# Selective scan: three of sixteen products with C on GpSimd, step sizes summed by TensorE, B's rows spread by DMA, eight states in the ring

## The chip, the cores and the metric

The kernel runs on one core of one Trainium2 chip. The metric is the device time of the whole program in microseconds (us); before the change the median of three runs is 4557.76 us (4557.75 to 4559.65). Engines are named as the profile names them: PE is TensorE, PEld its weight load, DVE is VectorE, ACT is ScalarE, POOL is GpSimd, SP is SyncE, which issues the transfers.

## The reference, cut to what matters

The program is a chain of eleven phases (three attentions, two mixtures of experts, two recurrent networks, norms, and one selective scan). Only the scan is touched. Its arithmetic, with 16 batch elements of 512 tokens, 256 inner channels and 16 states per channel:

```python
xz = jnp.einsum('btd,ed->bte', x, in_proj_w)
xi, z = jnp.split(xz, 2, axis=-1)
xc = _silu(causal_depthwise_conv(xi) + conv_b)
x_dbl = jnp.einsum('bti,ei->bte', xc, x_proj_w)
dt_lo, Bp, Cp = jnp.split(x_dbl, [DT_RANK, DT_RANK + D_STATE], axis=-1)
dt = jax.nn.softplus(jnp.einsum('btr,ir->bti', dt_lo, dt_proj_w) + dt_proj_b)
A = -jnp.exp(A_log)
def step(h, inp):
    dt_t, B_t, C_t, x_t = inp
    dA = jnp.exp(dt_t[..., None] * A[None])
    dBx = dt_t[..., None] * B_t[:, None, :] * x_t[..., None]
    h = dA * h + dBx
    y_t = jnp.sum(h * C_t[:, None, :], axis=-1)
    return (h, y_t)
y = scan(step) + Dp * xc
y = y * _silu(z)
return jnp.einsum('bti,di->btd', y, out_proj_w)
```

## The kernel before, in words

Two functions make the selective scan. `mamba_in` goes over the 16 batch elements, makes xc, silu(z), the raw step size and the 32 rows of B and C, and stores them to DRAM; B and C are stored as three bf16 parts whose sum is the f32 row (`high`, `middle`, `low`). `mamba_scan` then loads one batch element after another and runs 16 states n = 0 to 15 for each. Channels are the partitions, in two halves of 128 that lie side by side in a tile of 1024 columns (2 halves of 512 tokens). For state n of batch element b:

- PE spreads row n of B over 128 partitions (`broadcast_b`, L2247, into the PSUM tile `b_ps`), ACT copies it to SBUF (`copy_b`, L2323, `b_sb`).
- POOL multiplies it with dt*x, one instruction per half (L2449, `dbx`, ring of R = 4).
- ACT makes exp(dt*A) for both halves (L2363, `da`, ring of 2 in PSUM).
- DVE runs the recurrence with one scan instruction (L2498, `state`, ring of RS = 4).
- PE spreads row n of C (`broadcast_c`, L2253, one PSUM tile `c_ps`); it may do so once DVE has read the row before.
- DVE multiplies state and C (`times_c`, L2506, `prod`, ring of 2), one state behind the scan.
- PE adds the product to `y_ps` with a product with the identity matrix (`sums`, L2271).

Beside these, once per batch element: ACT and POOL make the next element's step size (six ACT instructions per half, L2330 to L2354, then `lose`, `mend`, `step_size` on POOL, L2422 to L2432) and POOL scales x by it (L2439); PE adds D*x to y at n = 9 and 11 (L2295); DVE gates y (L2515); PE multiplies by the output weights and adds the residual (`outward`, L2262 and L2263, at n = 4, into the same PSUM tile as B's rows); ACT copies the result (`take_sum`, L2350).

Each engine runs its own list in the order in which it is written in `sequence`; semaphores order the engines among each other. The order around the change is set by the constants at the head of `mamba_scan` and by the `if n == ...` lines in each `sequence`. Transfers are issued by SP in the order of `load`.

Of the kernel before, what the change touches and what calls it, by code (L numbers as in the profile page):

```python
# [1967 lines left out]
def mamba_in(core, xn, mamba_dram, bc_dram, w):  # L1968
# [7 lines left out]
    with core.phase() as ph:  # L1976
# [16 lines left out]
        STORES = 4  # L1993
# [7 lines left out]
        def _(pe):  # L2001
# [40 lines left out]
        def _(act):  # L2042
# [47 lines left out]
        def _(dve):  # L2090
# [11 lines left out]
            def copy_dbl(n):  # L2102
                dve.wait_ge(dbl_mm, n + 1)
                if n >= 1:
                    dve.wait_ge(dt_mm, 2 * n)
                dve.tensor_copy(dbl[:, :], dbl_ps[0:BC + RANK, :]).then_inc(dbl_copied, 1)

            def rest_of(n):
# [3 lines left out]
                dve.tensor_tensor(rest[:, :], dbl_ps[0:BC, :], high[:, n % OB], ALU.subtract).then_inc(rest_ready, 1)  # L2112
# [25 lines left out]
        def _(sp):  # L2138
            def store(n, u):
                sp.dma_start(mamba_dram[n].rearrange("k p t -> p k t"), out[:, u]).then_inc(stored[u], 16)  # L2140
                for r, part in enumerate((high, middle, low)):
                    sp.dma_start(bc_dram[n, r], part[:, u]).then_inc(stored[u], 16)
# [9 lines left out]
def mamba_scan(core, x, mamba_dram, bc_dram, w):  # L2152
# [5 lines left out]
    RS = 4  # L2158
    RP = 2
    RA = 2  # L2160
    RB = 8
    AHEAD = 6
    COPIED = 4
    AT = 4
    SKIP_AT = (9, 11)
    OUT_AT = 4
    with core.phase() as ph:
        inp = ph.sb("inp", [P, 2, KINDS, T])
        bc = ph.sb("bc", [3 * BC, 2, T], BF16)
# [6 lines left out]
        b_sb = ph.sb("b_sb", [P, RB, T])  # L2176
        skip_w = ph.sb("skip_w", [P, 2, P])
        dbx = ph.sb("dbx", [P, R, 2 * T])
        state, prod = ph.sb("state", [P, RS, 2 * T]), ph.sb("prod", [P, RP, 2 * T])
        gated = ph.sb("gated", [P, 2, T])  # L2180
        da = ph.ps("da", [P, RA, 2 * T])
        b_ps, c_ps = ph.ps("b_ps", [P, T]), ph.ps("c_ps", [P, T])
        y_ps = ph.ps("y_ps", [P, 2, T])
        out_ps = b_ps
        loaded = [ph.sem(f"loaded{u}") for u in range(2)]
        step_loaded = [ph.sem(f"step_loaded{u}") for u in range(2)]
        select_loaded = ph.sem("select_loaded")
# [14 lines left out]
        acc_mm = ph.sem("acc_mm")  # L2202
# [8 lines left out]

        @block.sync
        def _(sp):
            def load(b, u):
                sp.dma_start(inp[:, u, 4:6], mamba_dram[ds(b, 1), 4:6].rearrange("a k p t -> (a p) k t")
                             ).then_inc(step_loaded[u], 16)
                sp.dma_start(bc[:, u], bc_dram[ds(b, 1)].rearrange("a r c t -> (a r c) t")).then_inc(loaded[u], 16)
                sp.dma_start(inp[:, u, 0:4], mamba_dram[ds(b, 1), 0:4].rearrange("a k p t -> (a p) k t")
                             ).then_inc(loaded[u], 16)

            load(0, 0)
            sp.dma_start(w["select"], w["select_dram"]).then_inc(select_loaded, 16)
# [12 lines left out]
        def _(pe):
            pe.sem_inc(acc_mm, 2 * RP)
            pe.sem_inc(out_mm, 1)

            def inputs_loaded(b, u):
                pe.wait_ge(loaded[u], 32 * (b // 2) + 32 if isinstance(b, int) else 16 * (b - u) + 32)  # L2240

            def broadcast_b(b, u, n):

                if n == 0:
                    inputs_loaded(b, u)
                pe.wait_ge(b_ready, STATE * b + n + 1)
                pe.matmul(b_ps[:, :], w["select"][:, n], bc[:, u], start=True, stop=True).then_inc(b_mm, 1)  # L2247

            def broadcast_c(b, u, n):
                if n == 0:  # L2250
                    inputs_loaded(b, u)
                pe.wait_ge(prod_ready, RS + STATE * b + n)
                pe.matmul(c_ps[:, :], w["select"][:, STATE + n], bc[:, u], start=True, stop=True  # L2253
                          ).then_inc(c_mm, 1)

            def outward(b, follows=True):

                pe.wait_ge(gated_ready, 2 + 2 * b + 2)
                pe.wait_ge(added, b + 1)
                pe.wait_ge(b_ready, 1 + (STATE * (b + 1) + OUT_AT + AHEAD + 1 if follows else STATE * (b + 1)))  # L2260
                for h in range(2):
                    pe.matmul(out_ps[:, :], w["out_w"][:, h], gated[:, h], start=(h == 0), stop=False)  # L2262
                pe.matmul(out_ps[:, :], w["ident"], tok(x, b), start=False, stop=True).then_inc(out_mm, 1)  # L2263

            def sums(b, n, first):
                m = STATE * b + n
# [492 lines left out]
```

## Time and profile before

| | |
|---|---|
| median of 3 runs | 4557.76 us |
| the profiled execution, its own time | 4557.68 us |
| its span, first to last instruction | 4555.9 us |
| busy in the span: PE, DVE, ACT, POOL | 86%, 71%, 65%, 52% |
| `mamba_in` | up to 1172 us |
| `mamba_scan`: first scan, last scan | 1192.81 us, 2059.69 us |

Busy shares are means over eleven phases with different limits, so the stage of the change is read by itself: the busy times of the engines from 1193 to 2066 us, then the groups of instructions in it, then the instructions in order of time. A duration is that of one instruction alone; where instructions of one engine follow each other without a gap, the distance from start to start is what one costs, and it is somewhat shorter than its duration.

### The profile page before, as it was taken

What the parts mean: (1) busy time and instruction counts of PE and PEld (TensorE: products, weight loads), DVE (VectorE), ACT (ScalarE), POOL (GpSimd) and SP (SyncE); (2) the same over time, 40 slices, a digit from 0 to 9 for tenths busy, and PEclk for the clock granted to TensorE, in tenths of its full rate; (3) what the DMA queues carried; (4) which work ended last, traced back from release to release, by engine and by line L of the source; (5) the groups of instructions that cost most, each with busy time, mean ns of one, the idle gap of its engine ahead of it and who ended that gap; (6) DMA issues with size and microseconds to landing.
All of it is one profiled execution on the core that took longest, in us unless ns stands there. A gap on an engine that the chain in (4) does not pass through costs nothing. (4 is left out here: it accounts for less than half of the span.)

```text
span 4555.9 us, 92840 instructions
## 1 busy us (share of the span) xinstructions
PE 3902.2 (86%) x30083; PEld 1984.7 (44%) x30084; DVE 3239.7 (71%) x7596; ACT 2951.3 (65%) x5997; POOL 2373.4 (52%) x2953
## 2 busy tenths in 40 slices
PE   7599999899677777779879999996988699997897
PEld 4244444463222222226423333335984244443896
DVE  3588888448799999994459999982116688887013
ACT  7488888767666666666758888883334477775332
POOL 3266666211688899980321545454544336665452
PEclk9799999999899999999979999998998799998997
DMA  9533333004310000000263333334655534442666
GB/s 279 166 90 86 86 87 88 23 0 162 110 40 34 29 29 29 29 15 0 103 200 88 91 88 90 89 83 138 211 191 194 173 107 118 115 113 81 198 215 197
DMA packets 500325, 486.05 MB, mean 107 GB/s; under 512 B 160194, under 2 KB 434755, under 8 KB 499808
## 3 DMA queue, kind: packets, MB, share of 16 engines
q1 hardware_dynamic: 481744, 443.29, 32.4%
q0 software_dynamic: 18160, 37.42, 2.3%
q8 instruction: 230, 3.77, 0.4%
q14 instruction: 191, 1.56, 0.1%
HBM read 321.07 MB, written 159.42 MB: 105 GB/s over the span
## 5 line engine op out<-in xcount | busy, mean ns | idle before, releaser
L1668 ACT ACTIVATE p_probs<-p_t_ps 128x512 f32<-128x512 f32 (+1 forms) x2048 | 1028.9, 557 | 345.8 <-PE p_t_ps L1427 149.4
L1448 PE MATMUL p_o_ps<-p_probs,p_v_st 128*32 128x256 f32 (+3 forms) x9728 | 749.8, 381 | 10.8 <-ACT p_o_sb L1630 10.1
L1761 DVE TENSOR_REDUCE p_row_max<-p_s_ps 128x1 f32<-128x512 f32 x1024 | 632.8, 678 | 56.2 <-PE p_s_ps L1376 56.1
L2449 POOL TENSOR_TENSOR p_dbx<-p_dtx,p_b_sb 128x512 f32<-128x512 f32 x512 | 635.7, 1274 | 42.8 <-DVE p_state L2498 40.0
L1376 PE MATMUL p_s_ps<-p_s_k,p_s_q 48*128 48x512 bf16 (+3 forms) x3072 | 607.0, 335 | 49.0 <-DVE p_row_max L1758 35.1
L2498 DVE TENSOR_TENSOR_SCAN p_state<-p_da,p_dbx 128x1024 f32<-128x1024 f32 x256 | 584.7, 2284 | 21.0 <-issue 18.1
L1409 PE MATMUL p_t_ps<-p_t_q,p_t_k 50*128 50x512 bf16 (+3 forms) x3072 | 545.2, 333 | 50.1 <-DMA p_t_q<-shifts 20.0
L1758 DVE CUSTOM_DVE_ANT_0 p_tried<-p_s_ps,c_mask_row 128x512 bf16<-128x512 f32 (+3 forms) x1024 | 441.2, 485 | 85.4 <-PE p_s_ps L1376 78.0
L1758 DVE CUSTOM_DVE_ANT_0 p_tried<-p_s_ps,p_s_bias 128x512 bf16<-128x512 f32 (+3 forms) x1024 | 441.6, 481 | 82.1 <-PE p_s_ps L1376 80.4
L1312 POOL TENSOR_TENSOR p_probs<-p_probs,xn 128x384 f32<-128x384 f32 (+1 forms) x384 | 408.8, 1092 | 153.9 <-ACT p_probs L1666 153.6
L2271 PE MATMUL p_y_ps<-p_prod,c_ident 128*128 128x512 f32 x1024 | 484.4, 595 | 3.4 <-DVE p_gated L2515 3.4
L802 POOL DMA_INDIRECT weighed_rows<-p_y,p_raw x284 | 271.8, 957 | 291.4 <-DVE p_y L790 246.9
L790 DVE TENSOR_TENSOR p_y<-p_out_ps,p_raw 128x256 f32<-128x256 f32 x142 | 60.3, 425 | 503.4 <-PE p_out_ps L741 503.4
L772 ACT ACTIVATE p_hidden<-p_hid_ps 128x512 f32<-128x512 f32 x284 | 169.6, 597 | 316.3 <-PE p_hid_ps L730 316.3
L1409 PEld LDWEIGHTS p_t_ps<-p_t_q,p_t_k 50*128 50x128 bf16 x3072 | 166.8, 93 | 462.5 <-ACT p_probs L1668 229.9
L2363 ACT ACTIVATE p_da<-p_dt,p_rate 128x512 f32<-128x512 f32 (+1 forms) x512 | 330.6, 680 | 10.4 <-DVE p_state L2498 10.4
L2323 ACT ACTIVATE p_b_sb<-p_b_ps 128x512 f32<-128x512 f32 x256 | 152.2, 594 | 283.9 <-PE p_b_ps L2247 245.4
L1448 PEld LDWEIGHTS p_o_ps<-p_probs,p_v_st 128*32 128x32 f32 x9728 | 194.1, 108 | 309.6 <-issue 256.1
L1376 PEld LDWEIGHTS p_s_ps<-p_s_k,p_s_q 48*128 48x128 bf16 x3072 | 213.6, 95 | 221.4 <-DVE p_row_max L1761 123.4
L2506 DVE TENSOR_TENSOR p_prod<-p_state,p_c_ps 128x1024 f32<-128x1024 f32 x256 | 306.3, 1196 | 0.5 <-PE p_c_ps L2253 0.5
L593 POOL DMA_INDIRECT routed_rows<-p_rows,p_index x256 | 251.8, 984 | 100.2 <-issue 72.9
L1303 POOL COPY p_v_st<-p_v_raw 128x128 f32<-128x128 f32 x192 | 55.7, 290 | 434.5 <-PE p_o_ps L1448 258.1
(308 smaller groups left out, 7205.3 us busy)
## 6 DMA issues: line engine op xcount, KB each, us to landing
p_wb<-in_w SPq DMA_DIRECT2D x142, 512.0 KB, 3.6
p_s_q<-stack_q SPq DMA_DIRECT2D x384, 96.0 KB, 2.3
p_s_k<-stack_k SPq DMA_DIRECT2D x384, 96.0 KB, 2.4
p_t_q<-stack_q SPq DMA_DIRECT2D x384, 96.0 KB
p_t_k<-stack_k SPq DMA_DIRECT2D x384, 96.0 KB
mamba_inputs<-p_out SPq DMA_DIRECT2D x16, 1536.0 KB, 5.6
p_raw<-routed_rows SPq DMA_DIRECT2D x142, 130.0 KB, 3.1
stack_q<-p_parts SPq DMA_DIRECT2D x48, 384.0 KB, 2.8
```

The lines of the kernel that those rows point to most:

```text
L1312: pool.tensor_tensor(tile, tile, bias["t_whole"][:, 4 * g + j, first - c * P:first - c * P + width], ALU.add).then_inc(t_biased, 1)
L1376: mm = pe.matmul(s_ps[:, slot, at:at + width], s_q[rows, g % 2, pair, c * P:(c + 1) * P], s_k[rows, g % 2, pair, 0:width], start=True, sto ...
L1409: mm = pe.matmul(out[r], t_k[rows, g % 2, pair, c * P:(c + 1) * P], t_q[rows, g % 2, pair, first:first + width], start=True, stop=not mask ...
L1448: mm = pe.matmul(o_ps[32 * j:32 * j + 32, at:to], v_st[:, g % 2, c, j, :], probs[:, g % 2, j, place[c] + at - first:place[c] + to - first] ...
L1668: act.activation(exps, tile, ACT.Exp, scale=scale).then_inc(expd, 1)
L1758: read = dve.tensor_tensor_reduce(tried[:, slot, at:at + width], scores, over, 1.0, LOWEST, ALU.add, ALU.max, found)
L1761: read = dve.tensor_reduce(found, scores, X, ALU.max)
L2271: pe.matmul(y_ps[:, h], w["ident"], prod[:, n % RP, half(h)], start=(n == 0), stop=(n == STATE - 1)).then_inc(acc_mm, 1)
L2363: act.activation(da[:, n % RA, h * T + h:h * T + T], dt[:, u, h, h:T], ACT.Exp, scale=rate[:, h, n:n + 1]).then_inc(da_ready, 1)
L2449: pool.tensor_tensor(dbx[:, n % R, half(h)], dtx[:, u, h], b_sb[:, n % RB], ALU.mult).then_inc(dbx_ready, 1)
L2498: dve.tensor_tensor_scan(out=state[:, n % RS], data0=da[:, n % RA], data1=dbx[:, n % R], initial=0.0, op0=ALU.mult, op1=ALU.add).then_inc( ...
L2506: dve.tensor_tensor(prod[:, n % RP].rearrange("p (h t) -> p h t", h=2), state[:, n % RS].rearrange("p (h t) -> p h t", h=2), c_ps[:, :].un ...
```

## The change

In `mamba_in` the rows of C alone are split into three bf16 parts; B and C are stored as f32 rows too (one more store, of `dbl`, which becomes a ring). In `mamba_scan`:

- B's rows come by transfers that read four rows of DRAM and write them to all 128 partitions (`load_b`, 1 MB each, four per batch element); `broadcast_b` and `copy_b` are gone.
- The products with C of the states 1, 6 and 11 (`BY_POOL`) are done by POOL, four states behind its own multiplication with B (`times_c` in its list), with rows of C that a transfer spreads (`load_c`, three of 256 KB). PE adds them three states later (`pool_sums`). DVE and `broadcast_c` leave these states out.
- The ring of states has eight places instead of four.
- The step size is a sum of four terms made by PE with the identity matrix (`step_sum`, four products per half at n = 5 and n = 7, into one PSUM tile that `outward` uses too); ACT copies it (`take_step`, at n = 9 and 11). `lose`, `mend` and `step_size` are gone from POOL. ACT's six instructions per half move from n = 4 to 11 to n = 0 to 6; `outward` moves from n = 4 to n = 3.
- SP's list is written out over the 16 batch elements, with a wait ahead of most transfers.

```diff
-    RS = 4
+    RS = 8
     RP = 2
     RA = 2
+    QUAD = 4
+    RB = 2 * QUAD
     SKIP_AT = (9, 11)
-    OUT_AT = 4
+    OUT_AT, TAKEN_AT = 3, 7
+    DT_AT, DT_COPIED_AT = (5, 7), (9, 11)
+    SCALED_AT = (13, 15)
+    BY_POOL = (1, 6, 11)
+    POOL_BEHIND, POOL_SUM_BEHIND = 4, 3
...
+            def load_steps(b):
+                if b >= 2:
+                    sp.wait_ge(above_ready, 2 * (b - 1))
+                sp.dma_start(inp[:, b % 2, 4:6], mamba_dram[b, 4:6].rearrange("k p t -> p k t")
+                             ).then_inc(step_loaded[b % 2], 16)
...
+            def load_c(b):
+                if b >= 1:
+                    sp.wait_ge(pool_prod_ready, K * b)
+                for j, n in enumerate(BY_POOL):
+                    sp.dma_start(c_sb[:, j], rows_dram[b, n:n + 1].to_broadcast([P, T])).then_inc(c_loaded, 16)
+            def load_b(b, q):
+                no = STATE // QUAD * b + q
+                if no >= 2:
+                    sp.wait_ge(dbx_ready, 2 * QUAD * (no - 1))
+                at = STATE + QUAD * q
+                sp.dma_start(b_sb[:, QUAD * (q % 2):QUAD * (q % 2) + QUAD].rearrange("p n t -> p (n t)"),
+                             rows_dram[b, at:at + QUAD].rearrange("n t -> (n t)").unsqueeze(0).to_broadcast([P, QUAD * T])
+                             ).then_inc(b_loaded[q % 2], 16)
+            load_steps(0)
+            load_steps(1)
+            load_inputs(0)
+            load_b(0, 0)
+            load_b(0, 1)
             sp.dma_start(w["select"], w["select_dram"]).then_inc(select_loaded, 16)
+            load_c(0)
+            load_inputs(1)
+            for b in range(NB):
+                if 1 <= b and b + 1 < NB:
+                    load_steps(b + 1)
+                load_b(b, 2)
+                if 1 <= b and b + 1 < NB:
+                    load_inputs(b + 1)
+                load_b(b, 3)
+                if b + 1 < NB:
+                    load_b(b + 1, 0)
+                    load_b(b + 1, 1)
+                    load_c(b + 1)
...
+            def step_sum(b, h):
+                pe.wait_ge(back, 4 * b + 2 * h + 2)
+                pe.wait_ge(soft, 1 + 6 * b + 3 * h + 3)
+                pe.wait_ge(above_ready, 2 * b + h + 1)
+                terms = (lost, small, log1, above)
+                for k, term in enumerate(terms):
+                    mm = pe.matmul(shared_ps[:, :], w["ident"], term[:, h], start=(k == 0), stop=(k == len(terms) - 1))
+                mm.then_inc(dt_mm, 1)
...
             def sequence(b, u, first=False, last=False):
                 for n in range(STATE):
+                    if n in BY_DVE:
+                        next_c(b, u, n, last)
+                        sums(b, u, n, first)
+                    if n - POOL_SUM_BEHIND in BY_POOL:
+                        pool_sums(b, u, n - POOL_SUM_BEHIND)
                     if n in SKIP_AT:
                         h = SKIP_AT.index(n)
                         pe.matmul(y_ps[:, h], skip_w[:, h], inp[:, u, h], start=False, stop=False)
                     if n == OUT_AT and not first:
                         outward(b - 1)
+                    if n in DT_AT and not last:
+                        h = DT_AT.index(n)
+                        if h == 0 and not first:
+                            pe.wait_ge(added, b + 1)
+                        if h == 1:
+                            pe.wait_ge(dt_ready, 2 * (b + 1) + 1)
+                        step_sum(b + 1, h)
```

On PE, in the second batch element of before, the part around `outward` stands as follows (`p_b_ps` holds B's spread row or the outward sum, `p_c_ps` C's row, `p_y_ps` the sum over states):

```order
L2271 MATMUL p_y_ps<-p_prod,c_ident 128x512 x2
L2262 MATMUL p_b_ps<-p_gated,c_out_w 128x512 x2
L2263 MATMUL p_b_ps<-x,c_ident 128x512
L2253 MATMUL p_c_ps<-p_bc,xn 128x512
L2271 MATMUL p_y_ps<-p_prod,c_ident 128x512 x2
L2247 MATMUL p_b_ps<-p_bc,xn 128x512 x2
L2253 MATMUL p_c_ps<-p_bc,xn 128x512
```

Behind the three products of `outward` the next row of C comes at once, and the states after it hold two short products and one pair of sums each.

In the same batch element of the changed kernel PE has this from n = 7 to n = 9 (L2297 spreads C's rows for n = 8, 9 and 10; `p_shared_ps` is the tile of the step sum; L2338 adds POOL's product; L2350 is D*x):

```order
L2297 MATMUL p_c_ps<-p_bc,xn 128x512
L2332 MATMUL p_y_ps<-p_prod,c_ident 128x512 x2
L2324 MATMUL p_shared_ps<-p_lost,c_ident 128x512
L2324 MATMUL p_shared_ps<-p_small,c_ident 128x512
L2324 MATMUL p_shared_ps<-p_log,c_ident 128x512
L2324 MATMUL p_shared_ps<-p_above,c_ident 128x512
L2297 MATMUL p_c_ps<-p_bc,xn 128x512
L2332 MATMUL p_y_ps<-p_prod,c_ident 128x512 x2
L2297 MATMUL p_c_ps<-p_bc,xn 128x512
L2332 MATMUL p_y_ps<-p_prod,c_ident 128x512 x2
L2338 MATMUL p_y_ps<-p_pool_prod,c_ident 128x512 x2
L2350 MATMUL p_y_ps<-p_inp,p_skip_w 128x512
```

The row of C for n = 9 now stands behind two sums and four products of the step size; the same four stand at n = 5.

On POOL, from the last third of the first batch element of before (`p_dbx` is the product with B, the other tiles are the step size):

```order
L2422 TENSOR_TENSOR p_lost<-p_small,p_lost 128x512
L2449 TENSOR_TENSOR p_dbx<-p_dtx,p_b_sb 128x512 x2
L2427 TENSOR_TENSOR p_log<-p_log,p_lost 128x512
L2449 TENSOR_TENSOR p_dbx<-p_dtx,p_b_sb 128x512 x2
L2432 TENSOR_TENSOR p_dt<-p_above,p_log 128x512
L2439 TENSOR_TENSOR p_dtx<-p_dt,p_inp 128x512
```

And one whole batch element of POOL's list in the changed kernel (the product with B is written to a part of `xn`):

```order
L2486 TENSOR_TENSOR xn<-p_dtx,p_b_sb 128x512 x12
L2495 TENSOR_TENSOR p_pool_prod<-p_state,xn 128x1024
L2486 TENSOR_TENSOR xn<-p_dtx,p_b_sb 128x512 x10
L2495 TENSOR_TENSOR p_pool_prod<-p_state,xn 128x1024
L2486 TENSOR_TENSOR xn<-p_dtx,p_b_sb 128x512 x6
L2476 TENSOR_TENSOR p_dtx<-p_dt,p_inp 128x512
L2486 TENSOR_TENSOR xn<-p_dtx,p_b_sb 128x512 x4
L2495 TENSOR_TENSOR p_pool_prod<-p_state,xn 128x1024
L2476 TENSOR_TENSOR p_dtx<-p_dt,p_inp 128x512
```

Six short instructions per batch element have gone from POOL's list and three of twice the width have come in.

## Rows read from the trace of the kernel before

**Rows 1.** Busy time of each engine in the scan stage, 1193 to 2066 us.

```profile
1193.00:2066.00 873.00, 658.65 (x1681) 253.94 (x1682) 868.38 (x542) 564.29 (x953) 776.61 (x630) 0.99 0.08 27
```

**Rows 2.** Groups in 1440 to 1660 us: line, engine, tiles, count | busy, mean ns | idle.

```profile
L2449 POOL TENSOR_TENSOR p_dbx<-p_dtx,p_b_sb 128x512 f32<-128x512 f32 x130 | 161.5, 1276 | 9.9 <-DVE p_state L2498 9.9
L2498 DVE TENSOR_TENSOR_SCAN p_state<-p_da,p_dbx 128x1024 f32<-128x1024 f32 x65 | 148.5, 2284 | 1.1 <-ACT p_da L2363 1.1
L2363 ACT ACTIVATE p_da<-p_dt,p_rate 128x512 f32<-128x512 f32 (+1 forms) x128 | 82.6, 680 | 0.0
L2506 DVE TENSOR_TENSOR p_prod<-p_state,p_c_ps 128x1024 f32<-128x1024 f32 x64 | 76.6, 1197 | 0.0
```

**Rows 3.** DVE in order of time: start, us, instruction.

```profile
1519.86 1.20 DVE L2506 TENSOR_TENSOR p_prod<-p_state,p_c_ps 128x1024 f32<-128x1024 f32 x1
1520.97 2.29 DVE L2498 TENSOR_TENSOR_SCAN p_state<-p_da,p_dbx 128x1024 f32<-128x1024 f32 x1
1523.17 1.20 DVE L2506 TENSOR_TENSOR p_prod<-p_state,p_c_ps 128x1024 f32<-128x1024 f32 x1
1524.28 1.28 DVE L2515 TENSOR_TENSOR p_gated<-p_y_ps,p_inp 128x512 f32<-128x512 f32 x2
1525.48 2.28 DVE L2498 TENSOR_TENSOR_SCAN p_state<-p_da,p_dbx 128x1024 f32<-128x1024 f32 x1
```

**Rows 4.** POOL in order of time: twelve multiplications with B in a run.

```profile
1512.31 14.77 POOL L2449 TENSOR_TENSOR p_dbx<-p_dtx,p_b_sb 128x512 f32<-128x512 f32 x12
```

**Rows 5.** Other two-operand POOL groups of the whole program, forms apart.

```profile
L555 POOL TENSOR_TENSOR p_rows<-p_raw,p_rstd 128x512 f32<-128x512 f32 x56 | 57.0, 1038 | 0.0
L1048 POOL TENSOR_TENSOR p_whole<-p_by_cos,p_by_sin 128x512 f32<-128x512 f32 x32 | 51.9, 1623 | 80.1 <-DVE p_by_sin L1003 78.2
```

**Rows 6.** PE in order of time around the outward products.

```profile
1538.87 0.39 PE L2253 MATMUL p_c_ps<-p_bc,xn 96*128 96x512 bf16 x1 [0.99 <-DVE p_prod L2506]
1539.10 1.88 PE L2271 MATMUL p_y_ps<-p_prod,c_ident 128*128 128x512 f32 x4
1540.82 1.88 PE L2262 MATMUL p_b_ps<-p_gated,c_out_w 128*128 128x512 f32 x4
1542.53 1.02 PE L2263 MATMUL p_b_ps<-x,c_ident 128*128 x2
```

**Rows 7.** The last row of C and the product that waited for it.

```profile
2061.89 1.20 DVE L2506 TENSOR_TENSOR p_prod<-p_state,p_c_ps 128x1024 f32<-128x1024 f32 x1
2063.14 0.39 PE L2253 MATMUL p_c_ps<-p_bc,xn 96*128 96x512 bf16 x1 [1.20 <-DVE p_prod L2506]
2063.63 1.22 DVE L2506 TENSOR_TENSOR p_prod<-p_state,p_c_ps 128x1024 f32<-128x1024 f32 x1 [0.54 <-PE p_c_ps L2253]
```

**Rows 8.** Transfers of 1250 to 1270 us: GB/s in 40 slices, size, us to landing.

```profile
GB/s 0 0 0 0 0 0 0 0 127 143 356 412 338 107 229 262 164 266 283 242 233 176 21 0 0 0 0 0 0 0 0 0 0 0 0 0 0 0 0 0
p_inp<-mamba_inputs SPq DMA_DIRECT2D x1, 1024.0 KB, 7.0
```

**Rows 9.** Transfers of 1172 to 1192 us: GB/s in 40 slices.

```profile
GB/s 0 0 0 131 94 373 399 395 373 389 377 352 451 434 279 213 262 213 221 209 291 387 371 262 365 385 389 393 254 12 0 0 16 0 0 0 0 0 0 0
```

**Rows 10.** Start of the scan stage in order of time.

```profile
1167.37 1.22 SPq L2142 DMA_DIRECT2D mamba_bc<-p_low  x1
1172.58 0.40 SPq L2215 DMA_DIRECT2D p_inp<-mamba_inputs  x1
1179.84 0.61 ACT L2346 ACTIVATE p_above<-p_inp 128x512 f32<-128x512 f32 x1
1183.66 0.61 ACT L2346 ACTIVATE p_above<-p_inp 128x512 f32<-128x512 f32 x1
1192.81 4.73 DVE L2498 TENSOR_TENSOR_SCAN p_state<-p_da,p_dbx 128x1024 f32<-128x1024 f32 x2 [18.10 <-issue]
```

**Rows 11.** Granted clock (seventh figure) as PE takes up its work.

```profile
1198.00:1200.00 2.00, 1.29 (x3) 0.69 (x4) 2.00 (x2) 0.87 (x2) 2.00 (x2) 0.50 0.00 0
1202.00:1204.00 2.00, 2.00 (x7) 0.93 (x6) 2.00 (x1) 1.39 (x3) 2.00 (x3) 1.00 0.00 0
```

More of the change, by code:

```diff
@@ L2141, in store @@
                 for r, part in enumerate((high, middle, low)):
-                    sp.dma_start(bc_dram[n, r], part[:, u]).then_inc(stored[u], 16)
+                    sp.dma_start(c_dram[n, r], part[:, u]).then_inc(stored[u], 16)
+                sp.dma_start(rows_dram[n], dbl[0:BC, u]).then_inc(stored[u], 16)
             for n in range(NB):
@@ L2236, in _ @@
             pe.sem_inc(acc_mm, 2 * RP)
+            pe.sem_inc(pool_acc_mm, 2 * 2)
             pe.sem_inc(out_mm, 1)
[L2239 to L2247, printed above, removed]
@@ L2249, in broadcast_c @@
             def broadcast_c(b, u, n):
                 if n == 0:
[L2251 to L2256, printed above, removed]
+                    inputs_loaded(pe, b, u)
+                pe.wait_ge(prod_ready, 1 + D * b + BY_DVE.index(n))
+                pe.matmul(c_ps[:, :], w["select"][:, n], bc[:, u], start=True, stop=True).then_inc(c_mm, 1)
@@ L2258, in outward, with next_c @@
+            def next_c(b, u, n, last):
+                d = BY_DVE.index(n) + 1
+                if d < D:
+                    broadcast_c(b, u, BY_DVE[d])
+                elif not last:
+                    broadcast_c(b + 1, 1 - u, BY_DVE[0])
+            def outward(b):
                 pe.wait_ge(gated_ready, 2 + 2 * b + 2)
-                pe.wait_ge(added, b + 1)
-                pe.wait_ge(b_ready, 1 + (STATE * (b + 1) + OUT_AT + AHEAD + 1 if follows else STATE * (b + 1)))
+                if isinstance(b, int) and b == NB - 1:
+                    pe.wait_ge(added, b + 1)
+                else:
+                    pe.wait_ge(dt_ready, 2 * (b + 1) + 2)
@@ L2261, in outward @@
                 for h in range(2):
[L2262 to L2266, printed above, removed]
-                pe.wait_ge(prod_ready, RS + m + 1)
+                    pe.matmul(shared_ps[:, :], w["out_w"][:, h], gated[:, h], start=(h == 0), stop=False)
+                pe.matmul(shared_ps[:, :], w["ident"], tok(x, b), start=False, stop=True).then_inc(out_mm, 1)
@@ new lines, in step_sum, with sums @@
+            def step_sum(b, h):
[6 more added lines that the diff above has]
+                mm.then_inc(dt_mm, 1)
+            def sums(b, u, n, first):
+                pe.wait_ge(prod_ready, 1 + D * b + BY_DVE.index(n) + 1)
@@ L2310, in _ @@
             sequence(NB - 1, 1, last=True)
-            outward(NB - 1, follows=False)
+            outward(NB - 1)
         @block.scalar
@@ L2403, in _ @@
                 positive(0, 0, h)
-            for n in range(COPIED):
-                copy_b(0, n)
+                take_step(0, 0, h)
             sequence(0, 0, first=True)
@@ L2466, in sequence @@
-                    if n == AT + 11:
-                        scale_input(b + 1, 1 - u, 1)
+                    times_b(b, u, n)
+                    if n - POOL_BEHIND in BY_POOL:
+                        times_c(b, u, n - POOL_BEHIND)
+                    if n in SCALED_AT and not last:
+                        scale_input(b + 1, 1 - u, SCALED_AT.index(n))
             for h in range(2):
-                lose(0, h)
-                mend(0, h)
-                step_size(0, 0, h)
                 scale_input(0, 0, h)
@@ L2518, in sequence @@
                 for n in range(STATE):
-                    scan(b, n)
-                    if n:
-                        times_c(b, n - 1)
-                    elif not first:
-                        times_c(b - 1, STATE - 1)
+                    scan(b, n, first)
+                    if n == 0 and not first:
+                        times_c(b - 1, 1 - u, STATE - 1)
+                    if n and n - 1 in BY_DVE:
+                        times_c(b, u, n - 1)
                     if n == 1 and not first:
```

267 lines of the change are left out of this document (123 added, 144 removed).

## The prediction

> **What bounds the kernel now.** The change touches one of eleven phases, so I read the busy times of the engines by stage first, then the groups inside the scan stage, then the order of time there. In the scan stage DVE is busy for 868.38 of 873 us; POOL has 776.61, PE 658.65 and ACT 564.29 [rows 1]. The groups say the same from the other side: DVE's scan and product idle for 1.1 us and 0.0 us in 220 us, while POOL idles only for DVE's scan [rows 2]. So DVE sets the pace, and each engine that gets more work has to be weighed against the new pace.
>
> DVE's price is read from start to start [rows 3]: a product costs 1520.97 - 1519.86 = 1.11 us, a scan 1523.17 - 1520.97 = 2.20, the two gates 1525.48 - 1524.28 = 1.20. A batch element costs 16 x 3.31 + 1.20 = 54.2 us, and 16 of them 867, which is the stage.
>
> **DVE's saving.** Three products of 16 leave DVE: 48 x 1.11 = 53.3 us over 16 batch elements. The new pace would be 54.2 - 3.3 = 50.9 us. What follows asks which engine can't follow it.
>
> **POOL hides its new products.** Its multiplications with B cost 14.77 us for twelve [rows 4], 1.23 each, so 32 cost 39.4. `lose`, `mend`, `step_size` go (six per batch element) and two scalings stay: 2.5. No POOL instruction of 1024 columns stands in the trace. Groups of 512 columns run from 1.04 to 1.62 us [rows 5], so twice that, 2.1 to 3.2 us, bounds one from both sides; I take 2.4, twice the 1.23 of the nearest row, which has the same types and the same DVE beside it. Three are 7.2 and POOL's list is 49.1 us, at the upper bound 51.5. In the new order it stands up to four states ahead of the scan and loses that lead where it has a product to do; with 49.1 it keeps a lead of one to two states at the turn of a batch element. Cost: 0, and the DVE stall that comes next gives POOL more room. The ring of eight makes this possible: a scan reuses a place eight states later, when POOL's product of it (four states behind) is done.
>
> **ACT loses work.** Sixteen copies of B's rows go, two copies of the step size come. Its step work falls on n = 0 to 6, with at most two instructions (3.82 / 6 = 0.64 each [rows 10]) beside the 2 x 0.68 of `da` [rows 2]: 2.7 us per state against 3.31. Cost 0, if the step inputs have come (second rival).
>
> **PE's order costs part of the gain.** This is the term that I think is easy to miss. PE's busy time gives no alarm (13 short products and 45 f32 ones), but its list is in order, and a row of C for DVE stands behind whatever was put ahead of it. Prices from start to start at full clock [rows 6]: a row of C 1539.10 - 1538.87 = 0.22; two sums 1540.82 - 1539.10 = 1.72; so an f32 product of 512 columns 0.86, `outward` three of them 2.58, a step sum four of them 3.44. From PE's start of a row of C to DVE's product is 2063.63 - 2063.14 = 0.49, and PE takes it up 0.05 after DVE's product before it has ended (2061.89 + 1.20) [rows 7]. I take the start of DVE's product of n = 3 as time 0. DVE alone would start its products at 3.31 (n = 4), 6.62 (5), 12.13 (7, since 6 is POOL's), 15.44 (8), 18.75 (9). PE in the order of the changed list, each entry not before DVE's product of that n is over (its start + 1.25):
> - n = 3 from 1.25: row of C 0.22, sums 1.72, outward 2.58, done 5.8.
> - n = 4: row for n = 5 at 5.8, there at 6.25, in time for 6.62. Sums, then POOL's product of n = 1 (1.72): done 9.4.
> - n = 5: row for 7 in time. Sums, step sum 3.44: done 14.8.
> - n = 7 (could have begun at 13.4): row for 8 there at 15.3, just in time for 15.44. Sums, second step sum: done 20.2.
> - n = 8: the row for n = 9 starts at 20.2 and is there at 20.7. DVE wanted it at 18.75: a stall of 1.9 us.
> - n = 9: row for 10 is in time again, and up to n = 12 PE catches up.
>
> ACT waits too: `take_step` after n = 9 can't run before 15.0, so `da` of n = 10 comes 0.5 us late, but that lies inside the 1.9. The first batch element has no outward, so its stall is 0.7; the last has no step sum, so none. 14 x 1.9 + 0.7 = 27.3 us given back. The bounds: nothing, if PE's lag were hidden by chance, and 14 x 3.0 + 1.5 = 43 if each of the seven stages of the lag is 0.15 late.
>
> **Start of the scan.** Now the first step size goes ACT, POOL; then it goes ACT, PE, ACT, PE, ACT, POOL, since `take_step` of half 0 stands ahead of half 1 on ACT and waits for PE. ACT's first half ends at 1179.84 + 0.61 = 1180.45 and a half takes 1183.66 - 1179.84 = 3.82 [rows 10]. PE's two step sums are eight records each of 0.43 at the upper clock level (2.4 GHz). The granted clock is 0.50 at 1198 us after an idle stretch and 1.00 from 1202 [rows 11], the lower level is 1.2 GHz; so a sum costs 3.4 to 6.9 us and both 6.9 to 13.8; I take 10, since PE is idle before each. Then 1180.45 + 3.9 + 10 + two copies 1.2 + scaling 1.23 + product with B 2.46 + some six hand-overs 0.6 = 1199.8 against 1192.81: 7 us later (3.9 to 10.8).
>
> **`mamba_in`.** One more store of 64 KB stands at the end of each SP round; the last four stores end the phase, and one costs SP 1.22 us [rows 10]: between 0 and 1.2, I take 0.6. The new wait for a stored buffer on DVE is three batch elements old. Cost 0.
>
> **Sum**, from the profiled execution's own 4557.68 us (the median of the runs is 0.1 above): 4557.7 - 53.3 + 27.3 + 7.0 + 0.6 = 4539.3. I forecast 4540 us, with 4526 to 4554 as its own range (stall 1.2 to 2.6 us per batch element, start 4 to 11).
>
> **Rivals.** First: PE's lag costs nothing, and the whole saving but the start arrives: 4557.7 - 53.3 + 7.6 = 4512. For it: DVE never waited for PE in the stage but for the last row (0.54 us [rows 7]), though outward made PE late there too. Against it: then one burst of 2.58 stood alone, and now 2.58 + 1.72 + 3.44 + 3.44 follow within five states.
>
> Second, slower: the spread rows come late. SP issues `load_steps` of the element after next only behind `load_b` and `load_c`, which wait for POOL's last products, and ACT's first step instruction stands at n = 0 ahead of `da` of n = 1. Counted from DVE's scan 0, with a pace of 50.9 + 1.9 = 52.8: DVE's scan 11 ends at 39.6 (eleven scans, nine products, the gates, the stall, its own 2.28), POOL's last product with B at 42.3, the one with C at 44.6. Then 1.05 MB of B, 0.79 of C and 0.52 of step inputs, 2.36 MB, must land by 54.1, so that ACT's 0.6 and 1.36 let scan 1 of the next element start on time at 56.1. At the start of the stage bytes flow some 1.2 us after SP's issue (1172.58 [rows 10], the fourth slice of 0.5 us [rows 9]); with 1.5 us for that and for the last receipt, this asks 2.36 MB / 10.3 us = 229 GB/s. The loads of before, 2 KB pieces from distinct rows, moved 350 to 410 GB/s in their better slices and 107 to 283 in the others [rows 8, 9], and 1 MB took 7.0 us [rows 8]. No transfer that reads one row 128 times stands in the trace. At 300 GB/s they land at 51.7, with 2.4 us to spare; at 150, at 59.5, so 5.4 late, 15 times: 4540 + 81 = 4621. It decides from 1.2 us of lateness (18 us of gain over 15), which is about 205 GB/s. I weigh 300 as likeliest, since the pieces are 8 KB instead of 2 KB.
> By the Trainium skill, page "DMA: Bandwidth & Descriptors", section "Latency and other measured facts", copies between HBM tensors whose rows lie 4 MiB apart fell to 103 GB/s, which the page puts down, as an inference, to streams in lock-step that meet on the same memory channels; 128 partitions that read the same 8 KB at once may be such a case. At that rate, as an estimate from the page, 2.36 MB take 22.9 us, land 12.6 us late and make 4540 + 15 x 12.6 = 4729. No run here shows it; the rows of before, whose partitions lie 2 KB apart, do not.
>
> Third, slower: POOL becomes the bound. It decides from the point where its list exceeds 52.8: a product with C of (52.8 - 41.9) / 3 = 3.6 us, over the upper bound of the rows. At 4.5 us the list is 55.4, 2.6 over: 16 x 2.6 = 42, 4582. Against it: POOL's multiplications kept 1.23 with DVE at work beside them [rows 4].
>
> **Chances.** Forecast 0.55, first rival 0.2, late rows 0.2, POOL 0.05. A difference under 0.2% (9 us, 4548.6 to 4566.9) can't be told from no change here. Of the forecast 0.47 lies below 4548.6 and 0.08 above; with the first rival faster is 0.67. Late rows split: 0.05 with little lateness end as no change, 0.15 as slower; POOL 0.01 and 0.04. Same 0.14, slower 0.19. The range leaves the upper half of the late rows out and ends at 4508 and 4585.
>
> **What would show it.** Right: DVE's product idles for PE's row of C, once per batch element at n = 9, about 1.9 us, 28 us in sum; the scan stage from first to last scan is some 26 us shorter; the first scan starts near 1200. The second rival shows as a wait of ACT's absolute value (first of the six step instructions) on the transfer of the step inputs and of DVE's scan on `da`; the third as DVE's scan waiting for POOL's product with B; the first as a DVE that waits for nothing. Wrong would be any wait of DVE on another engine that is longer than PE's.

## The result and the profile after

The changed kernel takes 4577.48 us (median of 7 runs, 4570.99 to 4580.30) beside 4559.65 for the kernel before on the same chip: a ratio of 1.0039 [1.0029, 1.0049], slower by 0.39% where 4540, faster, had been forecast. The time lies inside the whole range (4508 to 4585) and outside the forecast's own (4526 to 4554).

The profiled execution has a span of 4578.1 us against 4555.9. Where its 22.2 us arose, with the borders read from start to start of the same instructions:

| stretch | before, us | after, us | difference |
|---|---|---|---|
| phases ahead of `mamba_in` | 1036.7 | 1038.9 | +2.2 |
| `mamba_in` | 135.9 | 136.6 | +0.7 |
| load of the first inputs to first scan | 20.2 | 27.9 | +7.7 |
| first scan to last scan | 866.9 | 873.2 | +6.3 |
| last product with C to next phase | 8.5 | 10.4 | +1.9 |
| phases behind | | | +3.4 |

The first and the last row are phases that the change doesn't touch. The times of one kernel differ from run to run by as much (before: 4556 to 4564 us in 25 runs), so they say nothing. The fourth row decides: it was forecast at -26.

The waits come first: what each engine waited for in the scan stage, 1193 to 2100 us (us in total, times, longest).

```profile
DVE p_prod L2551 <- PE p_c_ps L2297: 54.8, 42, 2.2
ACT p_small L2386 <- DMA p_inp<-mamba_inputs: 26.1, 14, 4.2
DVE p_state L2543 <- POOL xn L2486: 25.9, 2, 25.8
DVE p_state L2543 <- ACT p_da L2423: 2.7, 14, 0.2
```

The third line is the wait for the very first product with B. Afterwards DVE doesn't wait for POOL. It waits for PE's rows of C, three times per batch element and not once, 54.8 us and not 27.3. That is the whole gain and more: -53.3 + 54.8 + 0.2 for `da` (2.7 beside 2.5 before) and 2.9 of three other waits give +4.6 of the +6.3; the rest is not assigned.

The stage as a whole (length, then busy time of PE, weight loads, DVE, ACT, POOL, then the granted clock), and the group of POOL's new products:

```profile
1203.00:2080.00 877.00, 753.94 (x1612) 279.13 (x1612) 816.63 (x493) 456.29 (x731) 778.97 (x589) 0.95 0.32 114
```

```profile
L2495 POOL TENSOR_TENSOR p_pool_prod<-p_state,xn 128x1024 f32<-128x1024 f32 x48 | 112.8, 2351 | 0.0
```

Beside [rows 1], DVE's busy time fell by 52 us in a stretch 4 us longer, PE's rose by 95, and the granted clock reads 0.95. Before it was 1.00 between 1215 and 2060 us; [rows 1] read 0.99 because they hold the start. A POOL product takes 2351 ns; 2.4 was taken.

One batch element on DVE, in order of time (start, us, instruction, wait ahead of it):

```profile
1480.89 1.28 DVE L2559 TENSOR_TENSOR xn<-p_y_ps,p_inp 128x512 f32<-128x512 f32 x2
1482.09 4.46 DVE L2543 TENSOR_TENSOR_SCAN p_state<-p_da,xn 128x1024 f32<-128x1024 f32 x2
1486.47 1.19 DVE L2551 TENSOR_TENSOR p_prod<-p_state,p_c_ps 128x1024 f32<-128x1024 f32 x1
...
1498.33 1.22 DVE L2551 TENSOR_TENSOR p_prod<-p_state,p_c_ps 128x1024 f32<-128x1024 f32 x1 [1.85 <-PE p_c_ps L2297]
...
1507.95 1.22 DVE L2551 TENSOR_TENSOR p_prod<-p_state,p_c_ps 128x1024 f32<-128x1024 f32 x1 [0.70 <-PE p_c_ps L2297]
...
1513.62 1.22 DVE L2551 TENSOR_TENSOR p_prod<-p_state,p_c_ps 128x1024 f32<-128x1024 f32 x1 [1.97 <-PE p_c_ps L2297]
```

The waits stand at n = 5, 8 and 9. The forecast had n = 9 alone, with the same size (1.9). So something made PE late before the step sums. PE in the same element:

```profile
1481.72 1.95 PE L2332 MATMUL p_y_ps<-p_prod,c_ident 128*128 128x512 f32 x4 [0.31 <-DVE xn L2559]
1487.72 0.60 PE L2297 MATMUL p_c_ps<-p_bc,xn 48*128 48x512 bf16 x1 [4.04 <-DVE p_prod L2551]
1488.25 3.78 PE L2332 MATMUL p_y_ps<-p_prod,c_ident 128*128 128x512 f32 x4
1491.96 0.60 PE L2297 MATMUL p_c_ps<-p_bc,xn 48*128 48x512 bf16 x1
...
1496.86 1.02 PE L2315 MATMUL p_shared_ps<-x,c_ident 128*128 x2
1497.81 0.39 PE L2297 MATMUL p_c_ps<-p_bc,xn 48*128 48x512 bf16 x1
1498.13 1.99 PE L2332 MATMUL p_y_ps<-p_prod,c_ident 128*128 128x512 f32 x4
1499.95 1.88 PE L2338 MATMUL p_y_ps<-p_pool_prod,c_ident 128*128 128x512 f32 x4
```

Two things differ from the prices of [rows 6]. First, the sums at 1488.25 cost 3.71 us (1491.96 - 1488.25), not 1.72; PE had idled 4.04 us before them. At that turn DVE does two gates and two scans in a row, since POOL takes the product of n = 1. Second, a row of C costs 0.32 from its start to the next (1498.13 - 1497.81), 0.09 more stand between the last identity product and its own start (1497.81 - 1496.86 - 0.86), and the sums behind it cost 1.82 (1499.95 - 1498.13) and not 1.72: 0.51 in all, not 0.22. The expectations below count 0.41 for it; they leave out the last part.

The granted clock (the figure behind the busy times) of the same stretch:

```profile
1484.00:1486.00 2.00, 0.00 (x0) 0.00 (x0) 2.00 (x2) 1.60 (x3) 2.00 (x3) 1.00 0.93 310
1486.00:1488.00 2.00, 0.28 (x1) 0.10 (x1) 2.00 (x3) 1.97 (x4) 2.00 (x2) 0.84 0.52 199
1488.00:1490.00 2.00, 2.00 (x3) 0.83 (x3) 2.00 (x2) 1.56 (x4) 1.72 (x3) 0.50 0.00 0
...
1494.00:1496.00 2.00, 2.00 (x5) 0.76 (x4) 2.00 (x2) 0.51 (x1) 1.75 (x2) 0.95 0.00 0
```

Here the clock falls while PE idles, to its lower level, 1.2 GHz, and PE works some 7 us at it, the sums of two states, before 2.4 GHz are back. The last two figures are the DMA share and GB/s. Not every batch element pays as much: behind the idle time the sums cost 3.7 us in six of fifteen, and 3.0 in nine, where the clock falls only after PE has taken up work again. One of the nine, whose row starts at 1322.39 behind an idle time of 4.11 us:

```profile
1322.71 3.01 PE L2332 MATMUL p_y_ps<-p_prod,c_ident 128*128 128x512 f32 x4
```

```profile
1322.00:1324.00 2.00, 1.61 (x4) 0.77 (x5) 2.00 (x2) 2.00 (x4) 2.00 (x2) 0.88 0.03 7
```

### The profile page after: what moved, and what is told of

Same layout as the page of the kernel before. It is cut to its first block and busy times, and to the rows that moved or that the text cites. A ratio compares the mean times of both kernels' runs of the same rounds, so it can differ in the third digit from the quotient of the medians.

```text
span 4578.1 us, 91829 instructions
## 1 busy us (share of the span) xinstructions
PE 4013.9 (88%) x30036; PEld 2016.5 (44%) x30036; DVE 3188.4 (70%) x7548; ACT 2843.6 (62%) x5773; POOL 2371.2 (52%) x2905
## 5 line engine op out<-in xcount | busy, mean ns | idle before, releaser
L2486 POOL TENSOR_TENSOR xn<-p_dtx,p_b_sb 128x512 f32<-128x512 f32 x512 | 635.4, 1272 | 89.7 <-DVE p_state L2543 89.6
L2543 DVE TENSOR_TENSOR_SCAN p_state<-p_da,xn 128x1024 f32<-128x1024 f32 x256 | 578.9, 2276 | 28.6 <-POOL xn L2486 25.9
L2332 PE MATMUL p_y_ps<-p_prod,c_ident 128*128 128x512 f32 x832 | 443.8, 658 | 4.0 <-DVE xn L2559 4.0
L2551 DVE TENSOR_TENSOR p_prod<-p_state,p_c_ps 128x1024 f32<-128x1024 f32 x208 | 249.3, 1198 | 57.7 <-PE p_c_ps L2297 54.8
L741 PE MATMUL p_out_ps<-p_wb,p_hidden 128*128 128x128 f32 x2272 | 276.6, 275 | 0.0
```

The costliest lines, as they stand in the source:

```text
L741: mm = pe.matmul(out_ps[:, j % 2, c * P:(c + 1) * P], hidden[:, j % 2, f, c * P:(c + 1) * P], wb[:, j % WB, FFN + f * P:FFN + (f + 1) * P] ...
L2332: pe.matmul(y_ps[:, h], w["ident"], prod[:, prod_slot(u, n), half(h)], start=(n == 0), stop=(n == STATE - 1)).then_inc(acc_mm, 1)
L2486: pool.tensor_tensor(dbx[:, n % R, half(h)], dtx[:, u, h], b_sb[:, n % RB], ALU.mult).then_inc(dbx_ready, 1)
L2543: dve.tensor_tensor_scan(out=state[:, n % RS], data0=da[:, n % RA], data1=dbx[:, n % R], initial=0.0, op0=ALU.mult, op1=ALU.add).then_inc( ...
```

## Experiments

Each ratio below is to the kernel before on the same chip. Three causes could stand behind the 27 us of waits that were not forecast. **Clock:** the idle time at n = 1 halves the clock, PE is late from n = 3 on, and the outward product and the step sums find no room to catch up. **Row:** a row of C of 48 partitions costs 0.29 more than one of 96, up to 13 times per batch element. **Density:** both are small, and the list is simply too dense around n = 3 to 9.

**Keep PE busy at n = 1.** Four products that nobody reads run there.

```
+ if n == 1 and not first:
+     pe.wait_ge(dt_ready, 2 * b + 2)
+     for _ in range(4):
+         pe.matmul(shared_ps[:, :], w["ident"], inp[:, u, 0], start=True, stop=True)
```

> The changed kernel with four f32 products of 512 columns on PE at n = 1, into the tile of the step sum, which is free there; nobody reads them. They fill the 4.0 us in which PE waits after POOL's state n = 1. Theory A (the granted clock falls to 0.50 in that gap and the next two states run at half speed, which adds to PE's lag): the clock in the scan stage goes from 0.95 to 0.99 or more, DVE's wait for rows of C falls from 54.8 us to about 40 (2.75 us times 14), and the time by 15 us to about 4562. Theory B (only the order of PE's list makes the lag, the clock is without effect since PE is late anyway): 4577, wait unchanged.

Measured 4561.24 us, 1.0001 [0.9992, 1.0011]. PE in its trace at the same place, and DVE's wait:

```profile
1479.38 3.60 PE L2354 MATMUL p_shared_ps<-p_inp,c_ident 128*128 128x512 f32 x8
1483.58 0.39 PE L2297 MATMUL p_c_ps<-p_bc,xn 48*128 48x512 bf16 x1 [0.61 <-DVE p_prod L2555]
```

```profile
DVE p_prod L2555 <- PE p_c_ps L2297: 36.2, 27, 2.0
```

The idle time is 0.61 us, the granted clock 1.00 from 1215 to 2060 us, and the waits fall from 54.8 to 36.2: work that nobody needs makes the kernel 16 us faster. The clock's part is shown; what is left is still 9 over the forecast.

**A row of C from 96 partitions.** The rows of C are loaded twice, with zero weights for the second copy.

```
- bc = ph.sb("bc", [3 * STATE, 2, T], BF16)
+ bc = ph.sb("bc", [6 * STATE, 2, T], BF16)
```

> The changed kernel with the selection for C's rows padded from 48 to 96 partitions, as in the kernel before (lower half zero weights, C loaded twice). Theory A (a row of C costs PE 0.41 us from start to start where it was 0.22, because its tile of 48 partitions stands between tiles of 128): the row costs 0.22 again, the lag behind five rows shrinks by 0.95 us per batch element, DVE's wait falls by about 13 us, time about 4564. Theory B (the dearer row comes from something else, such as the clock): no change, 4577.

Measured 4550.11 us, 0.9979 [0.9969, 0.9988]. PE in its trace, and DVE's wait:

```profile
1488.60 1.02 PE L2317 MATMUL p_shared_ps<-x,c_ident 128*128 x2
1489.46 0.38 PE L2299 MATMUL p_c_ps<-p_bc,xn 96*128 96x512 bf16 x1
1489.68 1.88 PE L2334 MATMUL p_y_ps<-p_prod,c_ident 128*128 128x512 f32 x4
1491.40 1.88 PE L2340 MATMUL p_y_ps<-p_pool_prod,c_ident 128*128 128x512 f32 x4
```

```profile
DVE p_prod L2553 <- PE p_c_ps L2299: 29.7, 25, 1.6
```

Twice the rows, and the product is cheaper: 1489.68 - 1489.46 = 0.22, with no gap ahead, and the sums behind it cost 1.72 again (1491.40 - 1489.68), the prices of [rows 6]. The idle 4.04 us and the low clock are still there (0.95). The row's part is shown as well, and it is the larger one. Its size was missed: the wait fell by 25.1 us where 13 had been expected; that each row gave back 0.29 and not 0.19 is a part of it. By the Trainium skill, page "TensorEngine Tiling (Array Packing)", section "Key Properties", a change of the tiling mode drains TensorE, and by the list in its section "Available Configurations" a row of 48 partitions would fit a tile of 64 rows and one of 96 would not. The price of 0.51 against 0.22, with a part of it on either side of the row, agrees with it. That the partitions make the price is shown; the drain itself is not.

**Both.** Is the sum of the two all of it?

```
+ if n == 1 and not first: (the four unread products)
+ bc = ph.sb("bc", [6 * STATE, 2, T], BF16)
```

> The changed kernel with both single repairs of PE's prices, none of its order: the four unread products at n = 1 that keep the clock up, and the selection over 96 partitions. Theory A (the forecast's timetable of PE was right and only its two prices, full clock and 0.22 us per row, were not met): DVE waits for rows of C once per batch element, before the product of n = 9, for about 1.9 us, 27 us in sum, clock 0.99 or more, time about 4549. Theory B (the two repairs add up, 18.6 and 25.1 us less): a wait of 11 us, 4533.

Measured 4543.56 us, 0.9962 [0.9948, 0.9976]. DVE in its trace, and its waits:

```profile
1492.86 2.29 DVE L2549 TENSOR_TENSOR_SCAN p_state<-p_da,xn 128x1024 f32<-128x1024 f32 x1 [0.19 <-ACT p_da L2429]
1496.72 1.22 DVE L2557 TENSOR_TENSOR p_prod<-p_state,p_c_ps 128x1024 f32<-128x1024 f32 x1 [1.57 <-PE p_c_ps L2299]
```

```profile
DVE p_prod L2557 <- PE p_c_ps L2299: 22.5, 15, 1.6
DVE p_state L2549 <- ACT p_da L2429: 3.1, 15, 0.4
```

With the two prices that the forecast had used, DVE waits as it had forecast: once per batch element, at n = 9, 1.57 us, 25.6 us in all with `da` (27.3 forecast). First to last scan is 836.0 us, 31 under before. So the order of the list costs what the forecast had put on it, and density is no third cause of the 27 us. The two parts are not additive (18.6 and 25.1 alone, 32.3 together); a row of C that comes half a microsecond early should gain nothing more.

**The second step sum later.** Density.

```
- DT_AT, DT_COPIED_AT = (5, 7), (9, 11)
+ DT_AT, DT_COPIED_AT = (5, 11), (9, 14)
```

> The changed kernel with the second step sum at n = 11 instead of 7, copied by ACT at n = 14 instead of 11. Theory A (PE's list is too dense between n = 3 and n = 8): the waits before the products of n = 8 and 9 (0.70 and 1.97 us) go, the one before n = 5 (1.85 us, from the low clock) stays: DVE's wait falls from 54.8 to about 20 to 28 us, time about 4545. Theory B (the low clock alone makes all waits): the wait only moves behind n = 11, 4577.

Measured 4568.32 us, 1.0019 [1.0009, 1.0029]; the wait is 39.6 us. DVE in its trace, the waits of one element:

```profile
1489.28 1.22 DVE L2551 TENSOR_TENSOR p_prod<-p_state,p_c_ps 128x1024 f32<-128x1024 f32 x1 [1.33 <-PE p_c_ps L2297]
...
1498.89 1.22 DVE L2551 TENSOR_TENSOR p_prod<-p_state,p_c_ps 128x1024 f32<-128x1024 f32 x1 [0.70 <-PE p_c_ps L2297]
...
1515.61 1.22 DVE L2551 TENSOR_TENSOR p_prod<-p_state,p_c_ps 128x1024 f32<-128x1024 f32 x1 [0.90 <-PE p_c_ps L2297]
```

The wait at n = 9 is gone, but those at n = 5 and 8 stay, and a new one comes at n = 13, where the moved sum meets the skip products of n = 11. A miss: 20 to 28 us of wait had been expected.

**The outward product earlier**, into the idle time at n = 1.

```
- OUT_AT, TAKEN_AT = 3, 7
+ OUT_AT, TAKEN_AT = 1, 7
```

> The changed kernel with the outward products at n = 1 instead of n = 3, where PE waits. Theory A (dense list and low clock both): the gap of 4.0 us shrinks to about 1.4, the clock stays at 1.0, and 2.58 us leave the lag; DVE's wait falls from 54.8 to about 19 us (1.35 times 14), time about 4541. Theory B (clock without effect, order alone): about 2.58 of the lag goes, wait about 25, 4548; told apart by the granted clock. Theory C (late transfers or POOL set the pace): no change.

Measured 4538.93 us, 0.9955 [0.9938, 0.9971], with one number changed. PE in its trace, and DVE's wait:

```profile
1471.03 1.88 PE L2314 MATMUL p_shared_ps<-xn,c_out_w 128*128 128x512 f32 x4
1472.75 1.02 PE L2315 MATMUL p_shared_ps<-x,c_ident 128*128 x2
1475.23 0.39 PE L2297 MATMUL p_c_ps<-p_bc,xn 48*128 48x512 bf16 x1 [1.47 <-DVE p_prod L2551]
```

```profile
DVE p_prod L2551 <- PE p_c_ps L2297: 19.1, 13, 1.5
```

The useful 2.58 us now fill the idle time: 1.47 are left, the clock stays at 1.00, and the dense stretch behind is 2.58 us shorter. That is the filler's effect and a part of the density's in one edit.

**The start.** Both halves' logarithms ahead of either half's sums.

```
  for h in range(2):
      positive(0, 0, h)
+ for h in range(2):
      take_step(0, 0, h)
```

> The changed kernel, with both copies of the first step size on ACT behind the instructions of both halves, so that ACT makes half 1 while PE sums half 0. Theory A (the start is a chain ACT, PE, ACT, PE, ACT): one ACT half of 3.8 us leaves it and PE runs with less idle time ahead of its second sum, so the first scan comes 4 to 6 us earlier (1203.4 to about 1198), time about 4573. Theory B (the start waits for the spread rows of B, which are loaded behind 2 MB): no change.

Measured 4561.44 us (11 runs, 4553.99 to 4569.98), 1.0005 [0.9996, 1.0014]. The first scan starts at 1198.2 instead of 1203.4, as expected; the waits read 49.9 instead of 54.8. The profiled execution is the slowest of the eleven, 4569.98 us, and its 10 us under the changed kernel's profiled 4580.30 are these 5 + 5. The median gains some 15. The shorter executions had a higher mean granted clock (0.947 at 4553.99 us, 0.941 at 4569.98); why stays open.

**Input of the step size loaded first.** SP issues `load_steps` two elements ahead, in front of the loads that wait for POOL.

```
- if 1 <= b and b + 1 < NB:
-     load_steps(b + 1)
...
+ if b + 2 < NB:
+     load_steps(b + 2)
```

> The changed kernel with the step inputs of the element after next issued ahead of the spread rows of B and C instead of behind them. Theory A (ACT's 26 us of waiting for them is hidden): ACT's wait goes, the time stays at 4577. Theory B (the late step inputs delay PE's step sums and through them DVE): up to 26 us less, 4552.

Measured 4576.57 us, 1.0039 [1.0023, 1.0054]: no change from the changed kernel. ACT's 26.1 us of waits for the step inputs are gone, and DVE's wait for PE is 54.8 as before. So the late transfer cost nothing here.

**All repairs together**: outward at 1, step sums at 5 and 11, skip products at 3 and 13, rows of 96, the start. And the same without the rows of 96.

```
- SKIP_AT = (9, 11)
+ SKIP_AT = (3, 13)
(with OUT_AT = 1, DT_AT = (5, 11), DT_COPIED_AT = (9, 14), take_step in its own loop)
```

> The changed kernel with all moves together: outward at n = 1, second step sum at n = 11 and its copy at n = 14, D*x at n = 3 and 13 instead of 9 and 11, selection over 96 partitions, both first copies behind both halves. Theory A (PE's list and its clock are the whole loss): DVE waits for rows of C for less than 5 us, clock 0.99 or more, time 4577 - 55 - 5 = about 4518, 0.9% under the kernel before. Theory B (another engine takes over as soon as PE is out of the way: POOL with 49 us of 51 per batch element, or the step inputs): 4530 to 4560, with DVE's scan waiting for POOL or for ACT.

> The version with all moves, but with the selection over 48 partitions: outward at n = 1, second step sum at n = 11 and its copy at n = 14, D*x at n = 3 and 13, both first copies behind both halves. Theory A (with the order spread out PE has room, and the dearer row of 0.41 us is hidden but for n = 12, where the row stands behind the second step sum): DVE's wait under 10 us, time about 4510 to 4516. Theory B (the dearer row costs DVE in any order, 0.19 us times 208): 4547.

Measured 4506.65 us, 0.9888 [0.9872, 0.9903], and 4506.65 us, 0.9885 [0.9868, 0.9901]: 51 us under before, 71 under the changed kernel, and under what had been expected (4518, and 4510 to 4516). DVE's wait in the first of the two (the second reads the same):

```profile
DVE p_prod L2554 <- PE p_c_ps L2299: 0.5, 1, 0.5
```

The one wait left is that of the last row, as in [rows 7]. With PE's work spread out, the dear row costs nothing: it is priced only where PE is late.

**Four products for POOL** on top of all repairs, and then with the step inputs first.

```
- BY_POOL = (1, 6, 11)
+ BY_POOL = (1, 4, 8, 11)
```

> The version with all moves, and with four products of sixteen on POOL (states 1, 4, 8, 11) instead of three. DVE's list falls from 50.5 to about 49.8 - 0.4 = 49.4 us per batch element, POOL's rises to 39.4 + 2.5 + 4 x 2.31 = 51.1. Theory A (POOL becomes the bound): DVE's scan waits for POOL, the pace is 51.1 or more, time 4507 + 10 to 25 = about 4520. Theory B (POOL's list has slack that the trace hides): DVE's list sets the pace, 4507 - 17 = 4490.

> Four products on POOL as in the run before, with the step inputs issued ahead of the spread rows of B and C. Theory A (with four products ACT's wait of 73 us for the step inputs is what holds back da and with it DVE; they are issued behind POOL's last product): DVE's wait of 25 us for da goes, and the time falls from 4527 to between 4500 and 4512. Theory B (POOL's list of 51 us plus its wait of 2.4 us for the second step size is the bound, and ACT's wait only fills that time): the time stays within 5 us of 4527, with DVE waiting for POOL.

Measured 4526.55 us, 0.9923 [0.9906, 0.9939], and 4511.81 us, 0.9892 [0.9875, 0.9908]. Waits of the first of the two, then of the second:

```profile
ACT p_small L2388 <- DMA p_inp<-mamba_inputs: 73.3, 14, 9.0
DVE p_state L2546 <- ACT p_da L2425: 25.0, 24, 3.3
```

```profile
DVE p_state L2546 <- ACT p_da L2425: 7.5, 27, 0.4
```

Here the forecast's second rival appears: SP's loads stand behind POOL's last products, the step inputs come up to 9.0 us late for ACT, and DVE waits 25.0 us for `da`. With the inputs first, 15 us come back, but the 16 x 1.11 = 17.8 that a fourth product should bring over three don't come: the time stays 5 us above theirs. POOL in the second run, one batch element from scaling to scaling:

```profile
1499.80 1.26 POOL L2479 TENSOR_TENSOR p_dtx<-p_dt,p_inp 128x512 f32<-128x512 f32 x1
1501.03 14.79 POOL L2489 TENSOR_TENSOR xn<-p_dtx,p_b_sb 128x512 f32<-128x512 f32 x12
1515.78 2.34 POOL L2498 TENSOR_TENSOR p_pool_prod<-p_state,xn 128x1024 f32<-128x1024 f32 x1
...
1550.81 1.26 POOL L2479 TENSOR_TENSOR p_dtx<-p_dt,p_inp 128x512 f32<-128x512 f32 x1
```

POOL has no idle time in it: 51.0 us per batch element is POOL's own list (34 x 1.23 + 4 x 2.32 = 51.1). DVE turns at the same 51.0, though its list by [rows 3] is 49.7. So POOL is the bound with four products, at a pace that three had reached already (50.8 from gate to gate). This is read from the two equal paces: DVE's short waits are put down to ACT and PE, and no wait on POOL is seen after the first states.

## Why the forecast was wrong

**The step that failed** is "PE's order costs part of the gain". Its mechanism was right: DVE waits for rows of C that stand behind PE's other work. The term was mis-sized: 27.3 us where 54.8 came, at n = 5, 8 and 9 and not at n = 9 alone. It took [rows 6] for PE in the new list, a row of C at 0.22 and sums at 1.72, and let PE begin at n = 3 with time in hand and the clock up. Neither held. The 48-partition row costs 0.51. The wait of 4.04 us at n = 1 and its clock were left out: the working started behind it.

The trace of before could have been asked for all three. Two gates, two scans in a row and a product are 1.20 + 4.40 + 1.20 = 6.8 us of DVE [rows 3], in which PE has only 1.9 us of sums, begun after the first gate, so an idle time of some 4 us could be worked out; and [rows 11] showed what a long idle stretch does to the clock, which the forecast used for the start alone. And in `mamba_in` products with 8 partitions stand between products with 128:

```profile
1101.37 1.98 PE L2012 MATMUL p_z_ps<-xn,c_in_w 128*128 128x512 f32 x4
1103.29 1.98 PE L2028 MATMUL p_dt_ps<-p_dbl,c_dt_w 8*128 8x512 f32 x4
1105.19 1.98 PE L2006 MATMUL p_x_ps<-xn,c_in_w 128*128 128x512 f32 x4
```

The granted clock is 1.00 there, and yet two products cost 1.92 (1103.29 - 1101.37) and 1.90 (1105.19 - 1103.29), not the 1.72 of [rows 6].

With both prices put right by experiment the same list gives 4543.56 us against 4540, inside the forecast's own range.
By the Trainium skill, page "TensorE: Matmul & The Clock Gate", section "HAM oscillation — how this bites in real kernels", a loop whose every turn holds a long idle time of TensorE pays for the clock's return in each turn. The trace agrees: the clock reads 0.95 over the stage and sums cost 3.0 to 3.7 us once per element.

**DVE's saving**: right. 48 products left DVE, and without PE's lag the time fell by 51 us. First to last scan is then 808.6 us, 58 under before and not 53: a batch element of before takes 54.6 us from gate to gate where 54.2 had been worked out, since in twelve of them DVE waits 0.2 us for `da` and loses as much again in overlap. The versions with all moves don't have these waits.

**POOL**: right. 2.35 us per product beside 2.4, and no wait of DVE for it. The third rival has its point between three products and four.

**ACT**: right as to time. It waits 26.1 us for step inputs, which one experiment showed to be free.

**Start of the scan**: 7.7 beside 7.0. The two sums lasted 5.5 and 5.4 us to ACT's copy, hand-over included, so 10.9 beside 10. The first of them in order of time (1183.43 to 1188.91):

```profile
1183.43 2.05 PE L2324 MATMUL p_shared_ps<-p_lost,c_ident 128*128 128x512 f32 x2 [17.60 <-ACT p_above L2402]
1188.91 0.60 ACT L2410 ACTIVATE p_dt<-p_shared_ps 128x512 f32<-128x512 f32 x1 [5.62 <-PE p_shared_ps L2324]
```

**`mamba_in`**: 0.7 beside 0.6. **The end** was not in the sum: 1.9 us, since PE's sums of POOL's last product stand ahead of those of DVE's last one, and the gates wait for both.

**The second rival**: the spread rows did not come as slowly as it feared. Transfers from 1480 to 1540 us, GB/s in 40 slices:

```profile
GB/s 208 0 135 332 265 0 0 317 377 5 0 0 0 0 0 0 60 382 257 0 0 0 0 0 0 0 0 311 377 281 210 348 45 0 0 0 328 360 22 64
```

By SP's issues, transfers of B's rows alone are the bursts from 1490.5, 1505 and 1534 us: 317 to 382 GB/s in the slices that they fill (332 and 265 are the next element's inputs). The burst from 1520.5 us holds the forecast's 2.36 MB, rows of B and C and step inputs: 8.1 us, 291 GB/s, where 300 had been taken and 205 was the point from which it decides. Its order of events was real: with four products DVE waited 25.0 us for it, and loading the inputs first gave 15 us of time back. The 103 GB/s that the Trainium skill's page "DMA: Bandwidth & Descriptors", section "Latency and other measured facts", gives for rows 4 MiB apart were not what 128 reads of one row got.

**The chances** gave slower 0.19, all of it to late rows and POOL. That PE's lag might be twice as large had a bound of 43 us, and at that bound the sum is 4555, no change; a low clock inside the loop was in none of the cases.

## What to carry to other kernels

When work is taken off the engine that sets the pace, walk the next engine's list through one whole turn of the loop, beginning at its longest idle time, and price each entry at the clock that it will meet there and in the shape that it will have, not by the row before. If an idle time grows, look for useful work of the same engine that can stand in it: one number (the outward product at n = 1) was worth 39 us here. And ask at once which engine is the bound when the repair succeeds: POOL had room for three products, not for four.

## What the hardware showed that was not expected

- An idle time of 4.04 to 4.11 us inside a steady loop put the granted clock to 0.50, during it or behind it, in fifteen of the sixteen batch elements; the longest idle time of an element of the kernel before, 1.71 us, left it at 1.00. Four products that nobody reads, 3.60 us of work in that place, made the kernel 16 us faster.
- A product with 48 partitions between products with 128 takes 0.51 us of PE's time, 0.10 of it in the sums behind it; one with 96 takes 0.22, at the same 512 columns.
- Transfers in which 128 partitions read the same 8 KB of DRAM moved 317 to 382 GB/s in the slices of 1.5 us that they filled alone.
